# Recurrent cell with four weight sets: one round of the last chunk's products moved ahead of the choice, done for all four cells

## What is computed

```python
def step(carry, x_t):
    h, c = carry
    sel_in = jnp.concatenate([h, c, x_t], axis=-1)
    logits = sel_in @ W_sel.T + b_sel
    onehot = jax.nn.one_hot(jnp.argmax(logits, axis=-1), Sx, dtype=x_t.dtype)
    g_all = jnp.einsum('bi,sgi->bsg', x_t, W_ih) + jnp.einsum('bh,sgh->bsg', h, W_hh) + b_ih + b_hh
    g = jnp.einsum('bsg,bs->bg', g_all, onehot)
    h2, c2 = _lstm_activate(g, c)
    return ((h2, c2), h2)
```

## Time and profile before

| | us |
|---|---|
| median of three runs (lowest, highest) | 8031.54 (8022.19, 8033.26) |
| the profiled execution's own time | 8021.68 |
| its span in the profile | 8020.0 |
| part of the span in the recurrent loop after its first step | 3251.0 |
| TensorE busy, whole span | 7173.6 |

### The profile page before, as it was taken

One profiled execution on the slowest core, in us unless ns is written; L12 is line 12 of the kernel. 1 busy time (PEld: TensorE's weight loads), 2 busy tenths in 40 slices (PEclk: granted clock), 3 DMA queues, 4 the chain that ended last, 5 costly groups with the idle time before them and its releaser, 6 DMA issues. The chain is left out here.

```text
span 8020.0 us, 483127 instructions
## 1 busy us (share of the span) xinstructions
PE 7173.6 (89%) x209931; PEld 3982.8 (50%) x209931; DVE 2471.2 (31%) x12097; ACT 1713.7 (21%) x7668; POOL 697.0 (9%) x1191
## 2 busy tenths in 40 slices
PE   7889989999999999999798999999999999999851
PEld 5423244444444444444396555555555555555520
DVE  5267643211111111111243222222222222222247
ACT  0222222333333333333100111111111111111111
POOL 0134359100000000000000000000000000000000
PEclk9889999999999999999899999999999999999975
DMA  1133211000000000000031111111111111111100
GB/s 42 24 85 85 81 53 50 5 0 0 0 0 0 0 0 0 0 0 0 13 142 48 6 6 6 6 6 6 6 6 6 6 6 6 6 6 6 20 12 7
DMA packets 739824, 152.53 MB, mean 19 GB/s; under 512 B 694067, under 2 KB 708981, under 8 KB 739756
## 3 DMA queue, kind: packets, MB, share of 16 engines
q1 hardware_dynamic: 695596, 85.27, 7.2%
q0 software_dynamic: 40704, 45.90, 2.1%
q10 hardware_dynamic: 3456, 20.48, 0.6%
HBM read 123.19 MB, written 28.16 MB: 19 GB/s over the span
## 5 line engine op out<-in xcount | busy, mean ns | idle before, releaser
L988 PE MATMUL ode_busy<-ode_busy_x,ode_busy_w 128*32 128x320 f16 (+2 forms) x40000 | 2340.4, 311 | 44.7 <-issue 37.9
L1457 PE MATMUL ps_rows<-whh,h_pair 128*4 128x384 f16 x34944 | 1623.2, 326 | 18.6 <-issue 4.3
L1457 PEld LDWEIGHTS ps_rows<-whh,h_pair 128*4 128x4 f16 x34944 | 730.7, 84 | 698.4 <-issue 251.8
L982 PEld LDWEIGHTS ode_psa<-ode_a,ode_w2t 128*32 128x32 f32 x19968 | 410.4, 108 | 734.9 <-ACT ode_a L1037 578.9
L988 PEld LDWEIGHTS ode_busy<-ode_busy_x,ode_busy_w 128*32 128x32 f16 x40000 | 711.1, 95 | 57.1 <-issue 56.4
L1403 ACT COPY gate_rows<-ps_rows 128x384 f32<-128x384 f32 x624 | 298.3, 478 | 2057.6 <-PE ps_rows L1457 2057.6
L1378 DVE COPY gate_rows<-ps_rows_last 128x128 f32<-128x128 f32 x624 | 182.1, 292 | 1625.8 <-PE ps_rows_last L1457 1625.8
L1039 ACT ACTIVATE ode_b<-ode_psa 128x1 f32<-128x1 f32 x2496 | 427.2, 171 | 950.9 <-PE ode_psa L982 950.9
L982 PE MATMUL ode_psa<-ode_a,ode_w2t 128*32 128x1 f32 x19968 | 602.1, 180 | 0.0
L1037 ACT ACTIVATE ode_a<-ode_psu 128x1 f32<-128x1 f32 x1872 | 320.2, 171 | 726.4 <-PE ode_psu L982 726.4
L982 PE MATMUL ode_psa<-ode_ones,ode_b_parts 128*32 128x1 bf16 x9988 | 457.4, 163 | 0.0
(11 more groups left out here) (433 smaller groups left out, 8696.9 us busy)
## 6 DMA issues: line engine op xcount, KB each, us to landing
xg_buf<-xg_scratch SPq DMA_DIRECT2D x1248, 16.0 KB, 1.9
split_raw<-in_whh_t SPq DMA_DIRECT2D x32, 512.0 KB, 3.5
ig_w<-in_wih_t SPq DMA_DIRECT2D x8, 2048.0 KB, 10.6
xg_scratch<-ig_out ACTq DMA_DIRECT2D x16, 832.0 KB, 4.0
xg_scratch<-ig_out ACTq DMA_DIRECT2D x8, 836.0 KB, 3.6
msg_h<-h_scratch SPq DMA_DIRECT2D x88, 62.5 KB, 2.7
h_scratch<-mlp_h SPq DMA_DIRECT2D x40, 125.0 KB, 2.3
msg_snd<-up_scratch,msg_idx POOLq DMA_INDIRECT x176, 5.5
```

The source lines that it names most:

```text
L982: m = nc.tensor.matmul(ps[32 * j:32 * j + 32, 0:1], w[:, 32 * j:32 * j + 32], col, start=start, stop=stop, skip_group_check=True)
L988: nc.tensor.matmul(ps_busy[32 * j:32 * j + 32, 0:cols], busy_w[:, 32 * j:32 * j + 32], busy_x[:, 0:cols], start=True, stop=True, skip_grou ...
L1457: m = nc.tensor.matmul(out[32 * j:32 * j + 4, :], hpair[:, c, 2 - 2 * part:6 - 2 * part], whh[:, at + lo:at + hi], start=(part == 0 and c ...
```

## The change

TensorE does round (part 0, chunk 0) of the last chunk for all four cells ahead of its waits and its load, and leaves that round out of the chosen cell's code. psb then holds four ranges of 128 columns, one for each cell, in one bank; only cell 0's first matmuls carry the start flag. VectorE no longer knows by itself where the chosen cell's columns are, so it waits for its own `best`, loads the choice, branches, and copies from that cell's range. Nothing else in the program differs.

```diff
-                        v.wait_ge(S["rows_last"], k)
-                        nc.vector.tensor_copy(gsb[:, FIRST:D], psb[:, 0:D - FIRST]).then_inc(S["evac_v"], 1)
+                        v.wait_ge(S["best"], k)
+                        v.sem_inc(S["seen_v"], 1)
+                        s = v.value_load(code[0:1, 0:1])
+
+                        def move(e):
+
+                            v.wait_ge(S["rows_last"], k)
+                            nc.vector.tensor_copy(gsb[:, FIRST:D], psb[:, e * (D - FIRST):(e + 1) * (D - FIRST)]).then_inc(S["evac_v"], 1)
+
+                        with v.If(s < 1 << 16):
+                            with v.If(s < 1 << 8):
+                                move(3)
+                            with v.Else():
+                                move(2)
+                        with v.Else():
+                            with v.If(s < 1 << 24):
+                                move(1)
+                            with v.Else():
+                                move(0)
...
-                        def products(e, part, c, out, lo, hi):
+                        def products(e, part, c, start, out, lo, hi):
...
-                                                     start=(part == 0 and c == 0), stop=(part == 1 and c == KC - 1), skip_group_check=True)
+                                                     start=start, stop=(part == 1 and c == KC - 1), skip_group_check=True)
...
-                            return products(e, part, c, psg[:, e * BANK:e * BANK + FIRST], 0, FIRST)
+                            return products(e, part, c, (part, c) == (0, 0), psg[:, e * BANK:e * BANK + FIRST], 0, FIRST)
+
+                        def last(e, part, c):
+
+                            return products(e, part, c, (e, part, c) == (0, 0, 0), psb[:, e * (D - FIRST):(e + 1) * (D - FIRST)], FIRST, D)
 
                         pe.wait_ge(S["hp_ready"], k)
                         for c in range(AHEAD):
                             for e in range(CELLS):
                                 first(e, 0, c)
+                        for e in range(CELLS):
+                            last(e, 0, 0)
                         pe.wait_ge(xg_in[q], i * 32 + 32)
...
                             for part in range(2):
                                 for c in range(KC):
-                                    m = products(e, part, c, psb[:, 0:D - FIRST], FIRST, D)
+                                    if (part, c) != (0, 0):
+                                        m = last(e, part, c)
                             m.then_inc(S["rows_last"], 1)
```

## The result

The changed kernel takes 8294.08 us (four runs, 8285.81 to 8305.08) against 8031.59 before: the ratio is 1.033, with a 95% interval of 1.0312 to 1.0348. It is slower by 262 us. The forecast was no change, 8028 us, with a range up to 8180. One of the four executions of experiment 2 took 16725.61 us, twice the other three, for a reason that nothing here shows, and it is left out there.

What follows compares the result with a forecast made beforehand. The prediction took the 624-step loop as bound by stretches with different limits, including a hole in TensorE's stream; +0.045 - 0.05 us a step gave -3 us, 8019 profiled, 8028 us as median, range 8007 to 8180.

Steps and rivals of the forecast that it cites:

- the open term: TensorE's load of the choice: still starts 0.2 us behind best despite 96 instructions ahead; taken as 0.
- the sum: Per loop step: +0.045 us for added matmuls, -0.05 at turn(3), VectorE 0; -0.005 us, times 624 = -3 us.
- The rival for it: TensorE reaches its load of the choice later because room for issued instructions is limited; slower, chance 0.25.
- Its first form: TensorE's queue has room for 64, freed at a matmul's end: +0.225 us a step, +140 us, 8172 us.
- Its other form, a room of 36: TensorE issues only 36 instructions ahead: +0.385 us a step, +240 us, 8272 us; chance 0.1 above 8172.
- The added pairs' own time: 16 pairs ahead of the choice take 0.22 us; cost 0.01 behind a jump, 0.08 otherwise, mean +0.045 a step.
- the holes: Gaps in TensorE's stream before the chosen cell, 0.21 us behind a jump, 0.14 otherwise, that added matmuls would fill.
- The gain at turn(3): End of the products: VectorE's copy starts 0.056 us earlier, ending turn(3)'s wait; -0.05 us a step.
- VectorE's part at cost 0: VectorE's added wait, increment, load and branches hide in its 2.6 us idle before the copy; cost 0.
- A third load of the word: VectorE's load delays TensorE's by 0.08 us: +0.03 a step, +20 us, 8050 us; chance 0.15 together with longer jump.
- The longer jump back: VectorE's loop jump stalls another 0.12 us every second step: +37 us, 8065 us; chance 0.15 together with third load.

Runs made afterwards that it cites:

- experiment 2: Kernel before plus only the 16 added pairs of 128 columns ahead of TensorE's load, into columns nobody reads: 8335.65 us, ratio 1.0378.
- run 3: Kernel before plus 4 added pairs of 128 columns ahead of TensorE's load (72 instructions): 8029.84 us, ratio 1.0000.
- run 5: Kernel before plus 8 added pairs of 128 columns ahead of TensorE's load (80 instructions): 8133.33 us, ratio 1.0129.
- run 6: Kernel before plus 16 added pairs of 8 columns instead of 128 ahead of TensorE's load: 8329.59 us, ratio 1.0375.
- run 4: Changed kernel with the added round done by 4 matmuls of 512 columns instead of 16 of 128: 8030.30 us, ratio 1.0001 to the kernel before.
- run 11: Changed kernel with only the second round's 16 pairs at the stream's head cut from 384 to 96 columns: 8287.03 us.
- run 7: Changed kernel with all 32 pairs at the stream's head cut from 384 to 96 columns: 8074.83 us, ratio 1.0062 to the kernel before.
- run 12: Changed kernel with only the first round's 16 pairs at the stream's head cut from 384 to 96 columns: 8001.43 us, ratio 0.9971 to the kernel before.
- run 1: Kernel before plus only VectorE's wait, load and branches, TensorE unchanged: 8038.88 us, ratio 1.0012.

## Why the prediction was wrong

**The step that failed** is the one that the prediction called the open term, whether TensorE's load still starts on time. It took 0 there, "since neither kind of step shows the least dependence on how far the stream had got". That was true of the kernel before and proves only that 64 instructions do not reach the limit. Runs 2, 3, 5 and 6 show that 72 do not either, 80 cost 0.16 us and 96 cost 0.48 us, whatever their columns. The rest of the sum held: run 4, which has the change's products and columns with 72 instructions ahead instead of 96, came out at 8030, where the sum had 8028.

**What the limit is.** One rule gives the load in all runs without a jump: 64 instructions have room, an entry is freed when its matmul ends, 0.33 us behind its start as the profile models it, and the load comes 0.33 us later. With 96 instructions 32 must have left, the fourth group ends at 0.49 + 0.33 = 0.82, and the load comes at 1.15. With 80 it is the second group, 0.16 + 0.33 + 0.33 = 0.82, measured 0.83. With 72 it is the first, 0.66, which lies within best's own 0.67. In run 11 the first four groups are unchanged, and so is the load. In runs 7 and 12 the fourth starts at 0.13 and ends at 0.34, and best decides again. Behind a jump 0.43 us fit instead of 0.33.

The Trainium skill (TensorE: Matmul & The Clock Gate, section on the array of 16 sub-arrays, engine queue depths) gives 64 as the depth of TensorE's queue. With the rule above this case's traces agree with the number. The prediction had this number and let entries leave when they begin, and so placed the release 0.01 us behind best instead of 0.34.

The rule is argued from the fit, and the runs bound it only in part. A room of 60 to 64 instructions freed at their start, with a fixed 0.67 us to the load, is out: it gives 1.15 and 0.83 rightly, but in runs 7 and 12 it would put the load at 0.13 + 0.67 = 0.80 us without a jump, and it stands at 0.67. A release 0.17 us before the modelled end, when the next group starts, with 0.50 us from there to the load, fits all runs as well (0.65 + 0.50, 0.33 + 0.50, and 0.17 + 0.50 in runs 7 and 12). Counted in instructions not yet begun, with the weight loads one group ahead, this is a room of 52 to 59. Nor can any run tell 64 instructions from 32 pairs. Shown is that the number of instructions ahead decides, and that the first groups of the stream free the room.

**The rival for it** had the right place and direction, and limited room as its mechanism, at a chance of 0.25. Its first form put the release at 0.82 us, which is what fits, but it then took 0.93 us to the chosen cell, best's own distance in a stream that stands ready. Measured are 0.33 + 0.74 = 1.07 without a jump and 0.43 + 0.74 = 1.17 behind one. So it said 8172 and not 8294 us. Its other form, a room of 36, hit the time (8272) with a wrong mechanism, as run 11 showed. The range of 8180 cut off just this form.

**The added pairs' own time:** 0.22 us was right (0.22 in run 4), and so was their cost beside the holes: 4 wide in all steps give a net of 0, and in every second step -12.7 us in the trace against -12. By the median steps of run 4 the matmuls cost about 0.10 us in steps without a jump, where the prediction had 0.08 from a mean hole of 0.14; the hole of 0.11 that it had read in the one step was the typical one.

**The gain at turn(3):** right. The turns took 0.06 us less, and run 12 shows 24 us for 624 steps, 0.04 each. Run 2 against the changed kernel would give 0.067, so 0.05 lies between the two.

**VectorE's part at cost 0:** right to 8 us of 8030 (run 1). A third load of the word moved nobody else's, so this rival fell. The longer jump back is there but small: in the changed kernel VectorE's reduce starts 0.01 us later after the stream's start than before behind a jump (0.185 against 0.176 in the median), and without one as before (0.085 in both).

**Still open.** Why the release takes 0.10 us longer behind a jump; this was not tried. And why single steps need 0.79 or 0.88 us from load to chosen cell instead of 0.74: of the 312 steps behind a jump some 45 do so in the kernel before, so it does not come with the 96 instructions. What the load waits for inside the engine, beyond the count, is open as said above.

## What to carry to other kernels

A load or branch that an engine's own instruction stream must execute was reached in this kernel only when everything ahead of it had been issued, so count instructions there, not busy time. A hole in TensorE's stream that ends with "issue" is filled with few wide matmuls rather than many narrow ones: four of 512 columns left the time as it was, where sixteen of 128 cost 262 us. That a wait has slack at the present count says nothing on the next one; measure one value in between before taking it for zero.

## What was not expected of the hardware

The load's delay depends on how quickly the first matmuls of the stream finish, and not on those just ahead of the load: two kernels with the same instructions and columns, in another order, took 8287 and 8001 us. With TensorE's matmul row standing still for 0.78 us ahead of the chosen cell, behind a jump, the granted clock fell to the 1.2 GHz level for a part of 55 steps, which cost 68 us (run 7); with the same standstill run 11, whose head streams longer, kept a mean of 1.00 from 4400 to 7500 us. What makes the difference was not tried.
